# Routing of the mixture-of-experts tokens inside the second cross attention, step by step between its own steps

## What is computed

```
x = x + _L1_xattn_ref(_layernorm(x), ctx, ctx, Wq, Wk, Wv, Wo)   # 77 keys, 16 heads, causal
x = x + _L1_ffn_ref(_layernorm(x), gate_kernel, w0, w1, wo)

# _L1_ffn_ref: 64 experts, the best 2 for each token
gate_logits = einsum('te,ex->tx', x, gate_kernel)
weights, selected = top_k(gate_logits, 2)
weights = softmax(weights)
sorted_x = take(x, argsort(selected.reshape(-1)) // 2)
# then silu(sorted_x @ w0[e]) * (sorted_x @ w1[e]) @ wo[e] by expert, summed per token by weight
```

## Time and profile before

| | us |
|---|---|
| median of 3 runs | 5278.23 |
| lowest and highest | 5272.78, 5282.56 |
| profiled execution, its own time | 5269.54 |
| its span | 5267.5 |
| cross stage `xb`, first score matmul to last DVE instruction | 2936.1 to 3331.9 |
| route stage `ro` | 3333.8 to 3469.5 |
| expert stage `ex` | 3469.5 to the end |

### The profile page before, as it was taken

One profiled execution on the slowest core, in us unless ns is written; L12 is line 12 of the kernel. 1 busy time (PEld: TensorE's weight loads), 2 busy tenths in 40 slices (PEclk: granted clock), 3 DMA queues, 4 the chain that ended last, 5 costly groups with the idle time before them and its releaser, 6 DMA issues. The chain is left out here.

```text
span 5267.5 us, 120237 instructions
## 1 busy us (share of the span) xinstructions
PE 4990.4 (95%) x46960; PEld 3450.0 (65%) x46960; DVE 2863.8 (54%) x4878; ACT 1657.3 (31%) x2074; POOL 1684.1 (32%) x1428
## 2 busy tenths in 40 slices
PE   9999989989999999899989999869999999999998
PEld 4444446668886656444444555668789888878887
DVE  4243227766663355354542566556666666666665
ACT  1001015544232200234331344223433433333333
POOL 1000005545554211000002222444455445444443
PEclk9999999989999999999999999879999999999999
DMA  1000021231111233699987111335667777889996
GB/s 59 8 32 24 8 87 37 80 101 33 24 33 48 98 117 134 150 222 213 224 181 255 53 57 68 125 110 184 193 199 235 253 233 242 293 312 309 311 313 205
DMA packets 493727, 772.07 MB, mean 147 GB/s; under 512 B 119793, under 2 KB 263926, under 8 KB 492996
## 3 DMA queue, kind: packets, MB, share of 16 engines
q1 hardware_dynamic: 377360, 723.39, 42.5%
q0 software_dynamic: 36160, 43.09, 4.1%
q10 hardware_dynamic: 79988, 2.67, 1.0%
...
## 5 line engine op out<-in xcount | busy, mean ns | idle before, releaser
L3477 PE MATMUL ex_ps<-ex_w,ex_xT 128*32 128x256 f32 x20992 | 1232.3, 380 | 30.8 <-DVE ex_w L3378 23.8
L3477 PEld LDWEIGHTS ex_ps<-ex_w,ex_xT 128*32 128x32 f32 x20992 | 1013.0, 110 | 194.8 <-DVE ex_w L3378 30.5
L3378 DVE COPY ex_w<-ex_shelf 128x4096 f32 x328 | 749.7, 2286 | 327.5 <-PE ex_ps L3477 147.9
L3435 ACT ACTIVATE ex_w<-ex_shelf 128x4096 f32 x164 | 595.0, 3628 | 812.2 <-PE ex_ps L3489 690.6
L3489 PE MATMUL ex_ps<-ex_w,ex_hT 128*32 128x256 f32 x10496 | 654.2, 380 | 11.6 <-ACT ex_w L3435 6.1
L3489 PEld LDWEIGHTS ex_ps<-ex_w,ex_hT 128*32 128x32 f32 x10496 | 514.3, 110 | 96.8 <-issue 22.1
L3324 POOL DMA_INDIRECT ex_x<-moe_xn,ex_ix x328 | 532.4, 1623 | 136.8 <-issue 98.8
L3341 POOL DMA_INDIRECT out<-ex_y,ex_ix_out x164 | 312.5, 1906 | 821.6 <-DVE ex_xT L3365 328.6
L2766 POOL TENSOR_TENSOR go_xb<-go_xr,go_bias 128x2048 f32<-128x2048 f32 x8 | 38.2, 4776 | 720.6 <-DMA go_xr<-x 654.5
L617 PE MATMUL at_ps<-at_xT,at_kT 128*128 128x512 f32 (+3 forms) x640 | 239.3, 529 | 1.6 <-ACT at_kT L511 1.6
L617 PEld LDWEIGHTS at_ps<-at_xT,at_kT 128*128 128x128 f32 x640 | 116.7, 190 | 121.8 <-issue 109.1
...
## 6 DMA issues: line engine op xcount, KB each, us to landing
ex_shelf<-L_ffn_w SPq DMA_DIRECT2D x128, 2048.0 KB
...
cv_gt<-cv_g SPq DMA_DIRECT2D x320, 128.0 KB, 4.9
cv_vt<-cv_v SPq DMA_DIRECT2D x256, 128.0 KB, 5.1
...
```

Source lines behind the costliest of these rows:

```text
L3378: dve.tensor_copy(w_s[n][:, :], pick(shelf[n], buf)).then_inc(w_set[n].sem, 1)
L3435: act.activation(w_s[2][:, :], pick(shelf[2], buf), ACT.Copy).then_inc(w_set[2].sem, 1)
L3477: mm = pe.matmul(ps[r * LANES:(r + 1) * LANES, which, hh * FL:(hh + 1) * FL], xT[:, p % 2, k, hh * LANES:(hh + 1) * LANES], wu[which][:, k ...
```

## The change

Of the eight chunks' routing, seven move from the route stage into the loop of the cross stage. The transposes take `xn_o` where it lies in SBUF, so the loads of `moe_xn` in the route stage fall away (the stores remain, the experts gather from there). All PSUM traffic of the routing goes through bank 5, which `turn` uses already; ACT copies rows, logits and ranks from it to SBUF, and each user of the bank waits until ACT has taken its predecessor's data (`side`, `freed`). One row transpose lies in each even step from g = 12, logits of two tiles at u = 7 and u = 5, the first choice at u = 6, the second at u = 7, the ranks at u = 0, the count at u = 1, the places at u = 2 and 3, and two scatters in each of the steps u = 4 to 7. The loop runs to g = 75 in place of 73 on DVE and 72 on PE. Six chunks' scatters lie in the cross stage; those of the seventh and eighth, and all of the eighth's choices, ranks and places, stay in the route stage. There the order of the experts begins with three or four more small DVE instructions, since the counts come from the running sum and the matmuls of L3172 are gone. The table is cleared by a DMA from DRAM to DRAM at the start of the cross stage, where the routing's constants are loaded too, and PE waits for the constants before its loop. `choose_first`, `count_up`, `place` and `weigh` are the old code in functions, except that the choices read the logits from SBUF; they aren't repeated here.

```diff
@@ -776,9 +779,20 @@
         adds = lambda g: sum(1 for i in range(g + 1) if masked(i))
         turn_step = lambda c, t: (c - 1) * U + 1 + t
         q_step = lambda c, m: (c - 1) * U + 5 + m // 2 * 2
+        END = G + LO + 4 if onward else G + LO + 2
+        row_at = {2 * T + LO + 4: T for T in range(NT)} if onward else {}
+        logit_at = {min(k // 2 * U + LO + (13 if k % 2 else 7), G + LO + 3): k for k in range(NT // 2)} if onward else {}
+        CHOOSE = LO + 14
+        first_at, second_at, rank_at, count_at, place0_at, place1_at = (
+            {c * U + CHOOSE + n: c for c in range(NC - 1)} if onward else {} for n in (0, 1, 2, 3, 4, 5))
+        scatter_at = {c * U + CHOOSE + 6 + n: (c, n) for c in range(NC - 2) for n in range(TJ)} if onward else {}
...
         side, wide = [], []
-        for g in range(-U, G + LO + 1):
+        for g in range(-U, END):
+            if g in logit_at:
+                side.append(("logits", logit_at[g]))
+            if g in rank_at:
+                side += [("row", row_at[g]), ("rank", rank_at[g])]
...
+            if g in row_at and g not in rank_at:
+                side.append(("row", row_at[g]))
...
@@ -815,6 +833,8 @@
                 sp.dma_start(wo_s[:, :, :], weight_view(wo)).then_inc(wo_ld, 16)
             load_x(2)
             load_x(3)
+            if onward:
+                nxt.early(sp)
...
-                    if onward:
-                        sp.wait_ge(xn_o_st, 16)
-                        st.plain(sp)
-                    nxt.early(sp)
+                    if not onward:
+                        nxt.early(sp)
...
+                if g in scatter_at:
+                    c, n = scatter_at[g]
+                    for j in range(2 * (n % 2), 2 * (n % 2) + 2):
+                        nxt.scatter(pool, c, n // 2, j)
...
                 dve.wait_ge(rs_o_done, T + 1)
                 if t == 0 and c:
                     dve.wait_ge(xn_o_st, 16 * c)
+                if c:
+                    dve.wait_ge(nxt.t_mm, T - TJ + 1)
...
+                if onward and g == LO:
+                    nxt.begin(dve)
+                if g in first_at:
+                    nxt.choose_first(dve, first_at[g])
+                if g in second_at:
+                    nxt.choose_second(dve, second_at[g])
+                    nxt.pair(dve, second_at[g])
+                if g in count_at:
+                    dve.wait_ge(rank_kept, count_at[g] + 1)
+                    nxt.count_up(dve, count_at[g], rk)
+                if g in place0_at:
+                    nxt.place(dve, place0_at[g], 0)
+                if g in place1_at:
+                    nxt.place(dve, place1_at[g], 1)
...
+            def keep_row(T):
+                act.wait_ge(nxt.t_mm, T + 1)
+                if T >= 4:
+                    act.wait_ge(nxt.l_mm, (T - 4) // 2 + 1)
+                act.activation(rxT[:, T % 4].rearrange("p k t -> p (k t)"), ps[:, 5, :], ACT.Copy).then_inc(nxt.xT_done, 1)
+
+            def keep_logits(k):
+                c, t = k // 2, 2 * (k % 2)
+                act.wait_ge(nxt.l_mm, k + 1)
+                if c >= 2:
+                    act.wait_ge(nxt.both_done, c - 1)
+                act.activation(nxt.lg[:, c % 2, t:t + 2, :].rearrange("p t e -> p (t e)"), ps[:, 5, 0:2 * NE], ACT.Copy).then_inc(nxt.lg_done, 1)
+
+            def keep_ranks(c):
+                act.wait_ge(nxt.rank_mm, c + 1)
+                if c:
+                    act.wait_ge(nxt.rank_read, c)
+                act.activation(rk[:, :], ps[:, 5, 0:(TJ + 1) * NE], ACT.Copy).then_inc(rank_kept, 1)
...
+                if g in logit_at:
+                    keep_logits(logit_at[g])
+                if g in rank_at:
+                    keep_row(row_at[g])
+                    nxt.weigh(act, rank_at[g])
...
+            def turn_row(T):
+                n = side_at["row", T]
+                pe.wait_ge(xn_o_done, T + 1)
+                if n:
+                    pe.wait_ge(*freed(side, n - 1))
+                for k in range(KD):
+                    i = pe.transpose(ps[:, 5, k * P:(k + 1) * P], xn_o[:, T % TJ, k * P:(k + 1) * P], ident[:, :])
+                i.then_inc(nxt.t_mm, 1)
+
+            def logits(k):
+                n = side_at["logits", k]
+                pe.wait_ge(*freed(side, n - 1))
+                for t in range(2):
+                    T = 2 * k + t
+                    pe.wait_ge(nxt.xT_done, T + 1)
+                    for k_ in range(KD):
+                        i = pe.matmul(ps[:, 5, t * NE:(t + 1) * NE], rxT[:, T % 4, k_, :], nxt.gate[:, k_, :], start=k_ == 0, stop=k_ == KD - 1)
+                i.then_inc(nxt.l_mm, 1)
+
+            def rank_rows(c):
+                n = side_at["rank", c]
+                if n:
+                    pe.wait_ge(*freed(side, n - 1))
+                nxt.rank_rows(pe, c, ps[:, 5])
...
-            for g in range(G + LO + 1):
+            if onward:
+                pe.wait_ge(nxt.consts_in, nxt.ready)
+            for g in range(END if onward else G + LO + 1):
...
+                if g in logit_at:
+                    logits(logit_at[g])
+                if g in rank_at:
+                    turn_row(row_at[g])
...
+                if g in rank_at:
+                    rank_rows(rank_at[g])
+                elif g in row_at:
+                    turn_row(row_at[g])
...
     def early(sp):
-        sp.dma_start(st.x0[:, :, :], chunk_rows(xn_in[0:N, :], 0)).then_inc(st.x_in[0], 16)
         for k in range(KD):
             sp.dma_start(st.gate[k * LANES:(k + 1) * LANES], gate[k * P:(k + 1) * P, :].rearrange("(a i) e -> i a e", a=QUADS)).then_inc(st.consts_in, 16)
         for dst, src in ((st.ident, ident_d), (st.before, before_d), (st.token, token_d), (st.tiles, tiles_d)):
             sp.dma_start(dst[:, :], src).then_inc(st.consts_in, 16)
-        for dst, src in ((st.iota, iota_d), (st.region, region_d), (st.step_buf, buf_d), (st.ranks, ranks_d), (st.places, places_d), (st.pad, pad_d)):
+        for dst, src in ((st.iota, iota_d), (st.region, region_d), (st.step_buf, buf_d), (st.ranks, ranks_d), (st.places, places_d)):
             sp.dma_start(dst[:, :], src.to_broadcast([P, src.shape[1]])).then_inc(st.consts_in, 16)
-
-    st.early = early
+        sp.dma_start(table.rearrange("(p t) o -> p (t o)", p=P), pad_d.to_broadcast([P, pad_d.shape[1]])).then_inc(st.table_clear, 16)
+
+    def preset(pool):
+        pool.memset(st.ones[:, :], 1.0).then_inc(st.one_set, 1)
+        pool.memset(both[:, :, TJ, :], 0.0).then_inc(st.one_set, 1)
...
+    def begin(dve):
+        dve.wait_ge(st.consts_in, st.ready)
+        step(dve, dve.tensor_copy(at[:, :], st.region[:, :]))
+        for i in range(2):
+            step(dve, dve.tensor_copy(tw[:, i, :, 0], st.token[:, :]))
...
+    def choose_second(dve, c):
+        p = c % 2
+        step(dve, dve.scalar_tensor_tensor(lg[:, p], oh[:, p, 0], -3e38, lg[:, p], ALU.mult, ALU.add))
+        best(dve, c, 1)
...
+    def scatter(pool, c, i, j):
+        if j == 0:
+            pool.wait_ge(slot_done, 2 * c + i + 1)
+        if c == i == j == 0:
+            pool.wait_ge(st.table_clear, 16)
+        t = c * TJ + j
+        pool.indirect_dma_start(out=table, out_offset=bass.IndirectOffsetOnAxis(ap=slot[:, i, t:t + 1], axis=0),
+                                in_=tw[:, i, t, :], in_offset=None).then_inc(st.scattered[i], 16)
+
+    def rank_rows(pe, c, bank):
+        pe.wait_ge(st.both_done, c + 1)
+        p = c % 2
+        pe.matmul(bank[:, 0:TE + NE], st.before[:, :], both[:, p].rearrange("p t e -> p (t e)"), start=True, stop=False)
+        for t in range(TJ):
+            i = pe.matmul(bank[:, (t + 1) * NE:TE + NE].rearrange("p (t e) -> p t e", e=NE), st.ones[:, :],
+                          both[:, p, t:t + 1, :].to_broadcast([P, TJ - t, NE]), start=False, stop=t == TJ - 1)
+        i.then_inc(st.rank_mm, 1)
...
         def _(sp):
-            for c in range(1, RX):
-                sp.dma_start(x[c][:, :, :], chunk_rows(xn_d[0:N, :], c)).then_inc(x_in[c], 16)
-            sp.wait_ge(st.tail, 16 * 2 * TJ)
-            st.plain(sp)
-            sp.wait_ge(consts_in, 16 * (10 + KD))
-            sp.wait_ge(one_set, 3)
-            sp.dma_start(table.rearrange("(p t) o -> p (t o)", p=P), pad[:, :]).then_inc(table_clear, 16)
+            sp.wait_ge(zero_set, 1)
             sp.dma_start(xn_d[N:, :], zero[:, :]).then_inc(spare_clear, 16)
             sp.dma_start(out_d[N:, :], zero[:, :]).then_inc(spare_clear, 16)
-            for c in range(RX, NC):
-                sp.wait_ge(t_mm, part(c - RX, TJ - 1))
-                st.plain(sp)
-                sp.dma_start(x[c % RX][:, :, :], chunk_rows(xn_d[0:N, :], c)).then_inc(x_in[c % RX], 16)
             nxt.early(sp)
+            sp.wait_ge(st.tail, 16 * 2 * TJ)
             sp.wait_ge(spare_clear, 32)
             for i in range(2):
                 sp.wait_ge(scattered[i], 16 * NTL)
 
         @block.gpsimd
         def _(pool):
```

(20 more changed lines are left out.)

281 lines of the change are left out of this document (116 added, 165 removed).

## The result

The kernel before took 5275.6 us (median of 4 runs, 5272.8 to 5282.6), the changed kernel 5225.9 us (4 runs, 5217.4 to 5229.2): ratio 0.9897, 95% interval 0.9884 to 0.9909, that is 50 us less by the medians and 54 by the ratio, where 38 were forecast. The profiled execution of the changed kernel has a time of 5217.39 us and a span of 5215.4; against the profiled one of before (5269.54) that is 52.2 us less, where the forecast took it to 5231.5.

A forecast was written before the change was run, and what follows sets the result against it. PE was taken to bound the cross stage, chained waits and a half-speed PE the route stage. Cross +62.5 (42.8 + 4.0 + 5.2 + 10.5) and route -100.5 gave -38.0, 5278.2 to 5240.2 us, range 5222 to 5267.

The forecast's parts named there:

- Direction and the route stage: Faster, 5278.2 to 5240.2 us; the route stage was to go from 135.7 to 35.2 us, 100.5 less.
- Rows and logits: PE in the cross stage: 0.44 us a tile, 11.4; logits 1.83 a pair, 20.1, plus 1.3 in the last chunk.
- Ranks: PE in the cross stage: 2.0 us a chunk, 10.0 for five chunks.
- DVE late at u = 3, +4.0: Cross stage: DVE reaches the residual of u = 3 late, 0.8 us for each of five chunks, bounds 0 to 20.
- Everything else meets a full PE: Cross stage: outside the last chunk's bare odd steps, added PE work finds no idle PE time; no size of its own.
- The last steps and the tail: Cross stage from g = 64: 5.2 us up to the last output projection, +10.5 after it, ends +8 and +13.
- ACT, POOL, SP at nothing: Cross stage: added copies, scatters and constant loads on these engines cost nothing, at most 3 us for SP.
- Rival 1: PE's groups cost less, weight loads slipping under long matmuls; half of 26 us hidden gives 5227; chance 0.13.
- Rival 2: DVE becomes the bound of the cross stage, its choices held by POOL's products; +22 us gives 5262; chance 0.15.
- Rival 3: Cross stage: product waits behind two scatters, PE's transposes for the product; 60 us in all, 5300; chance 0.07.
- Rival 4: Gain given back: moved routing costs the cross stage twice the sum, or experts start later; 5275; chance 0.04.
- The rule behind rival 2: Cross stage: by an exclusive port lock, some dozen two-input choice operations a chunk could each wait for a POOL product.

The follow-up runs named there:

- The idle transposes: Kernel before with six idle transposes in the steps u = 0 and 2, behind or ahead of the output projection: 5229.1 and 5246.6 us on chip 3.
- the run with logits alone: Changed kernel with choices, ranks, places and scatters of all eight chunks back in the route stage, transposes and logits kept in the cross stage: 5287.9 us.
- the scatters' test: Changed kernel with all 64 scatters in the route stage, none between POOL's steps of the cross attention: 5281.3 us.

## Why the prediction was right or wrong

- **Direction and the route stage**: right. 35.7 us measured for 35.2, and the steps as listed: choices 5.5, ranks 4.2 with their wait, places 3.1. The medians' 5225.9 lies in 5222 to 5267, but at its low end; the profiled execution's 5217.4 lies below it, 14 us under the 5231.5 forecast for that execution. Of the 14, the cross attention with its tail makes 11.9 (50.6 for 62.5) and the stages that were not changed 2.7; the route stage gave 0.5 less than forecast.
- **Rows and logits**: right in price. 0.44 a tile and 1.78 a pair for 1.83. One of the two pairs in the last chunk's odd steps was mis-sized: at u = 7 no scores follow, so there is no wait to fill, and the step grew by 1.74 (the other by 0.64); 2.4 for 1.3. **Ranks**: 1.69 (the growth of u = 0, 2.12, less 0.44 for its row) for 2.0; 1.5 us over five chunks.
- **DVE late at u = 3, +4.0**: the step that failed. It was sized by DVE alone, and the wait that PE already had at u = 1 and 3 was held fixed. The same edit puts PE work behind the output projection, and there it covers the time in which DVE takes the residual, for which the next bare step used to wait. Up to g = 64 the growth is +36.7, where rows, logits and ranks at their measured prices make 11.4 + 19.6 + 2.4 + 8.5 = 41.9. So the term was -5.2, not +4.0, and outside the bounds of 0 and 20 that it was given. The steps themselves say the same: over the seven chunks from the second on, u = 1 is 3.9 us shorter than before and u = 3 is 1.2. With it 9 of the 12 us of error in the cross stage are told. The idle transposes show the mechanism by itself (0.65 us behind the projection: 0; ahead: +9.1). DVE's lateness is real but smaller, 0.3 to 0.4 us at u = 3 for 0.8, 1.4 in all by the run with logits alone. "Everything else meets a full PE" was false for one wait of 0.58 us that the prediction had itself read out.
- **The last steps and the tail**: 4.7 for 5.2 and 9.2 for 10.5. PE's clock was 0.57 from 3373 to 3377; the ranks took 3.4 us there (1.20 and 2.45, overlapping), between the forecast's 2.0 and 4.1.
- **ACT, POOL, SP at nothing**: right, for the scatters by experiment. For ACT the reason given, that an output projection lies between two users of bank 5, was right too: without it PE waited some 1.2 us three times a chunk.
- **Rival 1** (half the logits hidden): fell, 1.78 a pair. Its time, 5227, is nearer to the 5225.9 measured than the forecast's 5240, but that is chance: the time was lost and gained elsewhere. **Rival 2** (DVE the bound): fell, 4.2 us of waits in the stretch shown. **Rival 3** fell by the scatters' test. **Rival 4** fell: experts 1797.1 for 1798.0.
- **The rule behind rival 2**: by the port rule of the Trainium skill (SBUF — State Buffer, section "SBUF: two separate sides") a DVE operation with two SBUF inputs and a GpSimd one that reads SBUF shut each other out. Of all the routing's DVE operations with two inputs of 256 elements only one ran beside a POOL product:

```profile
3332.46 1.21 POOL L911 TENSOR_TENSOR xb_s<-xb_s,xb_rec 128x616 f32<-128x616 f32 x1
...
3333.47 0.49 DVE L3040 TENSOR_TENSOR ro_work<-ro_lg,ro_m 128x256 f32<-128x256 f32 x1
```

  It took 0.49 us in place of 0.42, a loss of 0.07. The order of the steps kept all the others apart from the products, so what a dozen such meetings would cost isn't shown. Beside POOL's small operations, which read SBUF too (L889, L898), such operations kept 0.39 to 0.43 us, so no loss of the size feared is seen there either. The rows that the prediction read as agreeing with the rule, gathers of 1623 ns and scatters of 971, are different instructions and show nothing of it.
- **What was not asked at all**: whether the route stage of before is 135.7 us everywhere. Its row shows a mean clock of 0.69 on a PE that begins at 1.00; that was taken as a property of the kernel. On chips 0, 3 and 7 kernels with the same routing need 112 to 116, and on the one of them where both were timed the change is worth 24 us in place of 47 to 54. That the forecast of 100 us for the route stage came true was in so far luck: the result came from the slow kind of chip, as the profile had.
